# Graph layer kernel, last six steps of the table loop: another bank for the turned rows, another order of work on three engines

## The chip, the cores and the metric

One core of a Trainium2 chip runs the whole program, in one launch. The metric is the device time of one execution in microseconds (us), lower is better. Engines are called by the names that the profile gives them: PE (TensorE, matrix products; PEld are its weight loads), DVE (VectorE), ACT (ScalarE), POOL (GpSimd, which here above all issues indirect DMAs), SP (SyncE, which issues plain DMAs).

## The reference, cut to what matters

The input is x, 3125 nodes of 256 float32 values, with 50000 edges (sorted by target node), an edge type (one of 3) for each edge and a node type (one of 6) for each node. The result is x plus three layers:

```
xn = layernorm(x)
x  = x + gnn(xn) + mix(xn)
x  = x + ffn(layernorm(x))         # only for the half of the nodes with the largest gate

gnn:  K, Q, V = xn @ W[node_type] + b[node_type]         # 256 -> 256 each, a weight matrix for each node type
      per edge type t: score = (K[src] Wa[t]) . Q[dst] * pri[t] / sqrt(32), softmax over all edges of the type,
      message = weight * V[src] Wm[t]; summed by dst, plus xn, layernorm
mix:  q, k, v = xn @ Wqkv.T; q, k = elu + 1; kv = k'v by head; t = q kv / (q . sum k)
      x1 = layernorm(t + xn); y = gelu(x1 @ W1.T + b1) @ W2.T + b2; layernorm(y + x1)
```

The change touches how the node tables K, V and Q times Wa are made, and how the last tiles of the mix layer are laid between them. What is computed stays the same.

## The kernel before, in words

The program is written out engine by engine. Each engine has a fixed list of instructions, and the order between engines is kept by semaphores: `then_inc` on an instruction counts up when it has ended, and `wait_ge` holds the engine that issues it, and all that stands behind it in its list. There is no planner; the order is that of the Python loops.

The first part (up to line 1310) reads x, normalises it, sorts the nodes into tiles of one type each (`NS` = 30 tiles of 128 slots, since a type's last tile is not full), and then runs **the table loop**: 31 steps, s = 0 to 30. In step s each engine does its share of table tile s (and of its neighbours s+1, s-1), and of the mix layer's tiles, of which there are only `NT` = 25, in a pipeline of six stages: mix tile s enters in step s, and tile s-5 leaves. So from step 25 on no new mix tile enters and the pipeline drains; the last mix tile leaves in step 29.

A table tile's way, by its lines: POOL loads its rows by an indirect DMA (`load`, L618, two steps ahead). PE turns them (`turn_in`, L883, two transposes, one step ahead) into PSUM bank ps[0]; ACT copies them out (`turn_in` of ACT, L714). PE multiplies them with the type's key and value weights (`keys_values`, L908, four products into ps[1]); DVE adds the bias (`kv_out`, L1227); POOL stores the tile by an indirect DMA (`store_kv`, L629). ACT copies the type's query weights (`weights`, L722). PE forms the queries (`queries`, L919), also in ps[0]; DVE adds their bias (`q_bias_in`, L1237), signalling g_qc. One step later PE multiplies them with the blocks of the edge types (`by_type`, L896), ACT copies the result (`q_out`, L732) and POOL stores it (`store_q`, L635).

Since queries and turned rows share ps[0], PE's `turn_in` of tile s+1 waits for g_qc of tile s. 

A mix tile's way: `mix_q` (L947, ps[2]), ELU on ACT and DVE (L760, L763, L1258, the last signals m_kf), `mix_t` (L959, ps[5]), `attend` on DVE (L1267 to L1276), `roots` on POOL (L644, L645), `shift` (L1250, DVE), `centre` (L752, ACT), `mix_turn` (L983, into ps[6]), `affine` (L771, ACT), `mix_h` (L972, ps[7]), `gelu` (L781, ACT), `mix_y` (L993 and L994, into ps[6] again), `residual` (L1284 to L1287 on DVE, reads ps[6], its last operation signals m_c), `roots` again, `finish` (L1293 to L1299, DVE), then SP stores the tile (L523). Two waits matter here, since mix_turn and mix_y share ps[6]: in step s the `mix_turn` of tile s-2 and the `mix_y` of tile s-4 both wait for m_c of tile s-5, which comes from the `residual` of that same step s.

The order of work within step s on each engine, before the change:

```
PE    mix_q(s)  keys_values(s)  mix_t(s-1)  mix_turn(s-2)  queries(s)  mix_h(s-3)  turn_in(s+1)  by_type(s-1)  mix_y(s-4)
DVE   residual(s-5)  kv_out(s)  elu(s)  q_bias_in(s)  attend(s-1)  finish(s-5)  shift(s-1)
ACT   centre(s-2)  elu(s)  affine(s-2)  weights(s+1)  gelu(s-3)  turn_in(s+1)  q_out(s-1)
POOL  roots(s-5)  gained(s-2)  load(s+2)  store_kv(s)  roots(s-1)  store_q(s-1)
```

After the loop, POOL waits for the key and value stores and for SP's first `s_end` (all mix tiles stored), and begins **the edge stage**: for each of 98 groups of edges four indirect gathers of 128 rows (L1406), 392 in all, while DVE, PE and ACT form scores, exponentials and window sums. SP's second `s_end`, after the last query store has landed, lets the other engines in. Then come the sums by node, the layer norms, the selection of nodes and the feed-forward layer (L2226, L2236).

Of the kernel before, what the change touches and what calls it, by code (L numbers as in the profile page):

```python
# [11 lines left out]
ACT = mybir.ActivationFunctionType  # L12
# [3 lines left out]
P = 128  # L16
N, D = 3125, 256
# [4 lines left out]
NT = -(-N // P)  # L22
# [44 lines left out]
def build(nc, a, out):  # L67
# [13 lines left out]
    with ExitStack() as ctx:  # L81
# [23 lines left out]
        ident = sb("ident", [P, P])  # L105
# [97 lines left out]
        xg = edge.take(2, D)  # L203
        xgT = edge.take(2, D)
# [123 lines left out]
        ps = [psum[:, i * 512:(i + 1) * 512] for i in range(8)]  # L328
# [35 lines left out]
        def seen(eng, event, tile, unit=1):  # L364
            if tile is not None and isinstance(event, list):
                eng.wait_ge(event[tile.k], unit * (tile.i + 1))
            elif tile is not None:
                eng.wait_ge(event, tile.t + 1)
# [42 lines left out]
        def type_marks(c, dve, in_t, tmp):  # L411
# [25 lines left out]
        g_T, g_Tc, g_w, g_kv, g_kvc, g_q, g_qc, g_qp, g_qpc = (  # L437
            sem(n) for n in ("g_T", "g_Tc", "g_weights", "g_kv", "g_kvc", "g_q", "g_qc", "g_qp", "g_qpc"))
# [9 lines left out]
        late_vecs = [name for name in vec_names if name not in mix_vecs]  # L448
        N_BIAS, N_LATE = 2 * NTY + len(mix_vecs) + 1, len(late_vecs) + 3
        PARTS, BY_DVE = (0, 5, 10, 15, NT), 10  # L450
        N_ROWS = 2 + len(vec_names) + 2

        with nc.Block() as block:
# [90 lines left out]
            def _(pool):  # L544
# [80 lines left out]
                def store_kv(t):  # L625
                    if t is None:
                        return
                    seen(pool, g_kvc, t)
                    pool.indirect_dma_start(kv_d[:, :], where(t), tab_kv[:, t.k, :], None).then_inc(g_kvout[t.k], 16)  # L629
# [9 lines left out]
                def roots(t, ready, done, n):  # L639
                    if t is None:  # L640
                        return
                    seen(pool, ready, t)
                    j = 2 * n + t.k
                    cm(pool.tensor_scalar(rss[:, j, 1:2], mvs[:, j, 1:2], EPS_LN, None, ALU.add))  # L644
                    pool.tensor_tensor(rss[:, j, 0:1], rss[:, j, 1:2], nhalf[:, 0:1], ALU.pow).then_inc(done, 1)  # L645

                def gained(t):
                    if t is None:
                        return
                    if t.t == 0:  # L650
                        pool.wait_ge(s_pri, 1)
                    seen(pool, m_xh, t)
                    seen(pool, m_c, t.at(-3))
                    pool.tensor_tensor(x1g[:, t.t % 3, :], xh[:, t.k, :], vecs["L0_mix_ln1_g"][:, :], ALU.mult).then_inc(m_xg, 1)
# [2 lines left out]
                load(Tile(0, 1, NS))  # L657
                for s in range(NS + 1):
                    t, m = Tile(s // 2, s % 2, NS), Tile(s // 2, s % 2, NT)
                    roots(m.at(-5), m_c, m_r2, 1)  # L660
                    gained(m.at(-2))
                    load(t.at(2))
                    store_kv(t.at(0))
                    roots(m.at(-1), m_tx, m_r1, 0)
                    store_q(t.at(-1))
                seen_all(pool, g_kvout, NS, 16)
# [2 lines left out]
            def _(act):  # L669
# [39 lines left out]
                def turn_in(t):  # L709
                    if t is None:  # L710
                        return
                    seen(act, g_q, t.at(-2))
                    seen(act, g_T, t)
                    act.activation(xgT[:, t.k, :], ps[0][:, 0:D], ACT.Copy).then_inc(g_Tc, 1)  # L714

                def weights(t):
                    if t is None:
# [78 lines left out]
            def _(pe):  # L796
# [80 lines left out]
                def turn_in(t):  # L877
                    if t is None:
                        return
                    seen(pe, g_qc, t.at(-1))  # L880
                    seen(pe, g_in, t, 16)
                    for ch in range(C):
                        ins = pe.transpose(ps[0][:, ch * P:(ch + 1) * P], xg[:, t.k, ch * P:(ch + 1) * P], ident[:, :])  # L883
                    ins.then_inc(g_T, 1)

                def by_type(t):
# [13 lines left out]
                def keys_values(t):  # L900
                    if t is None:
                        return
                    ty = pe.value_load(slot_tyi[0:1, t.t:t.t + 1], min_val=0, max_val=NTY - 1)
                    seen(pe, g_Tc, t)
                    seen(pe, g_kvc, t.at(-1))
                    settle(pe)
                    for ch in range(C):
                        ins = pe.matmul(ps[1][:, :], xgT[:, t.k, ch * P:(ch + 1) * P],  # L908
                                        wall[:, ds(ty, 1), ch, 0:2 * D].rearrange("p a o -> p (a o)"),
                                        start=(ch == 0), stop=(ch == C - 1))  # L910
                    ins.then_inc(g_kv, 1)

                def queries(t):
                    if t is None:
                        return
                    seen(pe, g_w, t)
                    for o in range(C):
                        for ch in range(C):
                            ins = pe.matmul(ps[0][:, o * P:(o + 1) * P], wq[:, t.k, ch * D + o * P:ch * D + (o + 1) * P],  # L919
                                            xgT[:, t.k, ch * P:(ch + 1) * P], start=(ch == 0), stop=(ch == C - 1))  # L920
                    ins.then_inc(g_q, 1)
# [29 lines left out]
                def mix_t(t):  # L951
                    if t is None:
                        return
                    if t.t == 0:
                        pe.wait_ge(s_kvd, 1)
                    seen(pe, m_kf, t)
                    seen(pe, m_tx, t.at(-1))
                    for ch in range(C):
                        ins = pe.matmul(ps[5][:, ch * 132:(ch + 1) * 132], qf[:, t.k, ch * P:(ch + 1) * P], kvd[:, ch, :],  # L959
                                        start=True, stop=True)  # L960
                    ins.then_inc(m_t, 1)
# [35 lines left out]
                for s in range(NS + 1):  # L997
                    t, m = Tile(s // 2, s % 2, NS), Tile(s // 2, s % 2, NT)
                    mix_q(m.at(0))
                    if s == 0:  # L1000
                        state_by_values()
                    keys_values(t.at(0))
                    mix_t(m.at(-1))
                    mix_turn(m.at(-2))
                    queries(t.at(0))
                    mix_h(m.at(-3))
                    turn_in(t.at(1))
                    by_type(t.at(-1))
                    mix_y(m.at(-4))

            @block.vector
            def _(dve):
# [288 lines left out]

                for s in range(NS + 1):
                    t, m = Tile(s // 2, s % 2, NS), Tile(s // 2, s % 2, NT)
                    residual(m.at(-5))
                    ty = kv_out(t.at(0))
                    elu(m.at(0))
                    q_bias_in(t.at(0), ty)
                    attend(m.at(-1))
                    finish(m.at(-5))
                    shift(m.at(-1))  # L1310
# [1209 lines left out]
```

## Time and profile before

| | |
|---|---|
| median of 3 runs | 1071.82 us (1071.51 to 1072.44) |
| the profiled execution | 1069.83 us, of which the span in the trace is 1068.1 us |
| busy share of the span | PE 82%, DVE 75%, POOL 60%, ACT 55% |
| mean granted TensorE clock | 0.888 of full |
| table loop, first keys and values to last query store | 80.1 to 289.5 us |
| the six changed steps (25 to 30) | from 256.54 us on |
| edge stage, first gather to the last | 289.96 to 780.9 us |

How to read it: each part of the table is a stretch of the same trace, in us from the span's start. The stages follow one another, and only their seams overlap, so a high busy share over the whole span does not tell what a single stage is waiting for. In the views of the trace, a number in square brackets is the time that the engine sat idle before the instruction, and the name behind it is what ended that wait. "issue" means that the profile shows nothing that it waited for.

### The profile page before, as it was taken

What the parts mean: (1) busy time and instruction counts of PE and PEld (TensorE: products, weight loads), DVE (VectorE), ACT (ScalarE), POOL (GpSimd) and SP (SyncE); (2) the same over time, 40 slices, a digit from 0 to 9 for tenths busy, and PEclk for the clock granted to TensorE, in tenths of its full rate; (3) what the DMA queues carried; (4) which work ended last, traced back from release to release, by engine and by line L of the source; (5) the groups of instructions that cost most, each with busy time, mean ns of one, the idle gap of its engine ahead of it and who ended that gap; (6) DMA issues with size and microseconds to landing.
All of it is one profiled execution on the core that took longest, in us unless ns stands there. A gap on an engine that the chain in (4) does not pass through costs nothing. (4 is left out here: it accounts for less than half of the span.)

```text
span 1068.1 us, 18060 instructions
## 1 busy us (share of the span) xinstructions
PE 880.7 (82%) x5049; PEld 634.7 (59%) x5049; DVE 806.2 (75%) x1708; ACT 588.5 (55%) x1532; POOL 638.9 (60%) x818
## 2 busy tenths in 40 slices
PE   5999999999657877777777777778777948999998
PEld 3776877877434444444444444444447937888886
DVE  6754788888568889898888898988866837886541
ACT  2655999997346666666666666666641213223220
POOL 4615777878677777777777777777720047672000
PEclk9999999999958788888878888887868969999999
DMA  9722344444588888888888888888826332110020
GB/s 284 252 82 90 135 163 146 144 146 153 170 262 252 249 247 250 246 250 254 246 248 254 248 249 252 249 248 252 254 69 242 107 115 70 50 48 4 1 94 27
DMA packets 111497, 189.61 MB, mean 178 GB/s; under 512 B 17861, under 2 KB 80140, under 8 KB 111396
## 3 DMA queue, kind: packets, MB, share of 16 engines
q0 software_dynamic: 38896, 129.86, 39.2%
q1 hardware_dynamic: 69220, 55.29, 16.8%
q10 hardware_dynamic: 3280, 3.28, 0.9%
q8 instruction: 43, 0.70, 0.3%
q14 instruction: 58, 0.48, 0.1%
HBM read 154.21 MB, written 34.16 MB: 176 GB/s over the span
## 5 line engine op out<-in xcount | busy, mean ns | idle before, releaser
L1406 POOL DMA_INDIRECT big<-kv_scratch,src_i x336 | 318.7, 949 | 102.1 <-issue 100.3
L1563 PE MATMUL ps<-edge 64*128 64x256 f32 x784 | 151.3, 519 | 16.2 <-DMA edge<-q_scratch 12.8
L1579 PE MATMUL ps<-big,edge 128*64 128x256 f32 x672 | 118.3, 484 | 37.2 <-DVE big L1748 21.1
L1689 DVE TENSOR_TENSOR big<-big,ps 128x1024 f32<-128x1024 f32 x84 | 102.4, 1219 | 41.0 <-DMA big<-kv_scratch,src_i 37.2
L1563 PEld LDWEIGHTS ps<-edge 64*128 64x128 f32 x784 | 89.5, 246 | 58.2 <-issue 47.7
L1579 PEld LDWEIGHTS ps<-big,edge 128*64 128x64 f32 x672 | 52.7, 167 | 85.5 <-DVE big L1748 43.1
L1477 ACT ACTIVATE edge<-edge 128x64 f32<-128x64 f32 x392 | 102.9, 334 | 0.0
L1696 DVE TENSOR_REDUCE ps<-big 128x32 f32<-128x1024 f32 x84 | 102.5, 1220 | 0.1
L1748 DVE TENSOR_TENSOR big<-big,ps 128x1024 f32<-128x1024 f32 x84 | 99.1, 1213 | 0.0
L2160 ACT ACTIVATE big<-ps,fb 128x256 f32<-128x256 f32 (+2 forms) x104 | 39.5, 462 | 101.9 <-PE ps L2226 101.9
L2226 PE MATMUL ps<-big 128*128 128x256 f32 (+2 forms) x416 | 91.0, 376 | 2.7 <-ACT big L2147 2.7
L2236 PE MATMUL ps<-big 128*128 128x256 f32 (+1 forms) x400 | 90.2, 380 | 1.2 <-ACT big L2160 1.2
L1499 ACT ACTIVATE edge<-ps 128x256 f32<-128x256 f32 x98 | 37.6, 384 | 91.3 <-PE ps L1579 89.7
L2226 PEld LDWEIGHTS ps<-big 128*128 128x128 f32 x416 | 76.6, 198 | 11.9 <-ACT big L2147 3.6
L2236 PEld LDWEIGHTS ps<-big 128*128 128x128 f32 (+1 forms) x400 | 73.6, 188 | 12.0 <-ACT big L2160 1.4
L1597 PE MATMUL ps<-ones,edge 128*96 128x1 f32 x196 | 27.6, 244 | 54.6 <-ACT edge L1490 54.6
L1406 POOL DMA_INDIRECT wmix<-kv_scratch,src_i x56 | 53.0, 946 | 17.1 <-issue 17.1
L1597 PEld LDWEIGHTS ps<-ones,edge 128*96 128x96 f32 x196 | 23.7, 186 | 66.0 <-ACT edge L1490 66.0
L908 PE MATMUL ps<-big,edge 128*128 x120 | 56.9, 596 | 0.5 <-ACT edge L714 0.3
L1462 ACT ACTIVATE edge<-edge,iota_n 128x256 f32<-128x256 bf16 x98 | 48.7, 497 | 13.3 <-DMA edge<-key_scratch 13.2
L1465 ACT ACTIVATE edge<-edge,ones 128x256 f32<-128x256 f32 x98 | 49.8, 508 | 9.2 <-PE ps L1563 0.4
L1481 ACT ACTIVATE edge<-edge,ones 128x256 f32<-128x256 f32 x98 | 49.8, 509 | 8.9 <-ACT edge L1477 0.4
(353 smaller groups left out, 1895.8 us busy)
## 6 DMA issues: line engine op xcount, KB each, us to landing
edge<-q_scratch SPq DMA_DIRECT2D x196, 64.0 KB
edge<-key_scratch SPq DMA_DIRECT2D x98, 64.0 KB
big<-kv_scratch,src_i POOLq DMA_INDIRECT x336
agg_scratch<-big SPq DMA_DIRECT2D x16, 252.0 KB
xn_scratch<-big ACTq DMA_DIRECT2D x5, 640.0 KB, 6.6
mix_scratch<-big SPq DMA_DIRECT2D x25, 128.0 KB, 1.7
edge<-mix_scratch SPq DMA_DIRECT2D x1, 3200.0 KB, 12.7
big<-xn_scratch SPq DMA_DIRECT2D x25, 128.0 KB, 2.5
```

The lines of the kernel that those rows point to most:

```text
L908: ins = pe.matmul(ps[1][:, :], xgT[:, t.k, ch * P:(ch + 1) * P], wall[:, ds(ty, 1), ch, 0:2 * D].rearrange("p a o -> p (a o)"), start=(ch ...
L1406: pool.indirect_dma_start(kv_slots[s][:, k, :], None, kv_d[0:N, :], bass.IndirectOffsetOnAxis(ap=src_i[:, e:e + 1], axis=0)).then_inc(got[ ...
L1465: act.activation(ohT[:, g % 2, :], dist, ACT.Relu, bias=ones[:, 0:1], scale=-1.0).then_inc(oh, 1)
L1477: ins = act.activation(gap[:, 2 * k + hg, :], iota_m, ACT.Abs, bias=neg_key[:, e:e + 1])
L1563: ins = pe.matmul(qr_ps[g % 2][:, (2 * hg + k) * D:(2 * hg + k + 1) * D], ohT[64 * hg:64 * hg + 64, g % 2, k * P:(k + 1) * P], qwin[64 * h ...
L1579: ins = pe.matmul(sums_of(g)[64 * hg:64 * hg + 64, :], oneh[:, s, k, hg * 64:hg * 64 + 64], kv_slots[s][:, 2 * hg + k, D:2 * D], start=(k ...
L1597: ins = pe.matmul(z_ps[:, b:b + 1], ex[:, b % 2, u * 4 * TH:(u + 1) * 4 * TH], ones[:, 0:1], start=(u == 0), stop=(u == 1))
L1689: dve.tensor_tensor(k_rows, k_rows, qr_ps[g % 2].rearrange("p (k d) -> p k d", d=D), ALU.mult).then_inc(pr, 1)
L1696: dve.tensor_reduce(scr[:, g // 2 % 2, (g % 2) * EG * H:(g % 2 + 1) * EG * H].rearrange("p (k h) -> p k h", h=H), kv_slots[g % RING][:, :, ...
L1748: dve.tensor_tensor(v, v, wgt[:, g // 2 % 2, (g % 2) * EG * H:(g % 2 + 1) * EG * H] .rearrange("p (k h d) -> p k h d", h=H, d=1).to_broadc ...
L2226: ins = pe.matmul(hslot[q % 2][:, j * GT * P:j * GT * P + w], fw1[:, ch, f * P:(f + 1) * P], cols[:, ch, at:at + w], start=(ch == 0), stop ...
L2236: ins = pe.matmul(ps[4 + t % 2][0:m, 0:D], fh[:, p % 2, f, at:at + m], fw2[:, f, :], start=(f == 0), stop=(f == FJ - 1))
```

## The change

It applies to steps s >= `NT` = 25 alone; steps 0 to 24 stay as they are.

- Turned rows of table tiles 26 to 29 go to bank ps[2], where the mix layer's queries stood (last used for mix tile 24 in step 24). PE's `turn_in` for them waits for all ELUs (m_kf) in place of g_qc of the tile before; the wait for g_qc moves to `queries`.
- PE's order in steps 25 and later: `keys_values(s)`, `turn_in(s+1)`, `by_type(s-1)`, `queries(s)`, and then `mix_t`, `mix_turn`, `mix_h`, `mix_y`.
- DVE: `residual(s-5)` moves from the head of the step to behind `q_bias_in(s)`.
- POOL: `roots(s-5)` and `gained(s-2)` move behind `load(s+2)` and `store_kv(s)`.
- ACT's order is not touched; its copy only reads from the other bank.

```diff
+        def after_mix_q(t):
+            return t.t > NT
+
+        def turned_ps(t):
+            return ps[2] if after_mix_q(t) else ps[0]
...
@@ pool
                 for s in range(NS + 1):
-                    roots(m.at(-5), m_c, m_r2, 1)
-                    gained(m.at(-2))
+                    if s < NT:
+                        roots(m.at(-5), m_c, m_r2, 1)
+                        gained(m.at(-2))
                     load(t.at(2))
                     store_kv(t.at(0))
+                    if s >= NT:
+                        roots(m.at(-5), m_c, m_r2, 1)
+                        gained(m.at(-2))
                     roots(m.at(-1), m_tx, m_r1, 0)
                     store_q(t.at(-1))
...
-                    act.activation(xgT[:, t.k, :], ps[0][:, 0:D], ACT.Copy).then_inc(g_Tc, 1)
+                    act.activation(xgT[:, t.k, :], turned_ps(t)[:, 0:D], ACT.Copy).then_inc(g_Tc, 1)
...
@@ pe
                 def turn_in(t):
-                    seen(pe, g_qc, t.at(-1))
+                    if after_mix_q(t):
+                        pe.wait_ge(m_kf, NT)
+                    else:
+                        seen(pe, g_qc, t.at(-1))
                     seen(pe, g_in, t, 16)
...
                 def queries(t):
                     seen(pe, g_w, t)
+                    if after_mix_q(t):
+                        seen(pe, g_qc, t.at(-1))
...
                     keys_values(t.at(0))
+                    if s >= NT:
+                        turn_in(t.at(1))
+                        by_type(t.at(-1))
+                        queries(t.at(0))
+                        mix_t(m.at(-1))
+                        mix_turn(m.at(-2))
+                        mix_h(m.at(-3))
+                        mix_y(m.at(-4))
+                        continue
                     mix_t(m.at(-1))
...
@@ dve
                 for s in range(NS + 1):
-                    residual(m.at(-5))
+                    if s < NT:
+                        residual(m.at(-5))
                     ty = kv_out(t.at(0))
                     elu(m.at(0))
                     q_bias_in(t.at(0), ty)
+                    if s >= NT:
+                        residual(m.at(-5))
                     attend(m.at(-1))
```

## Rows read from the trace of the kernel before

**Rows 1.** The page: the span, and the clock in 40 slices.

```profile
span 1068.1 us, 18060 instructions
...
PEclk9999999999958788888878888887868969999999
```

**Rows 2.** The page, costliest groups: busy us, mean ns, idle before.

```profile
L1406 POOL DMA_INDIRECT big<-kv_scratch,src_i x336 | 318.7, 949 | 102.1 <-issue 100.3
...
L1406 POOL DMA_INDIRECT wmix<-kv_scratch,src_i x56 | 53.0, 946 | 17.1 <-issue 17.1
```

**Rows 3.** Windows, steps 27, 28, 29 with tail: PE, PEld, DVE, ACT, POOL, clock, DMA.

```profile
270.23:275.97 5.74, 5.74 (x35) 4.21 (x34) 3.80 (x9) 2.29 (x8) 3.86 (x6) 1.00 0.62 190
275.97:281.71 5.74, 4.96 (x28) 3.32 (x27) 3.82 (x9) 1.78 (x5) 2.86 (x4) 1.00 0.55 193
281.71:289.96 8.25, 4.54 (x29) 2.87 (x27) 3.82 (x9) 1.84 (x5) 5.03 (x9) 0.93 0.43 164
```

**Rows 4.** Timeline, step 28 on PE: start, us, engine line op, idle before.

```profile
275.97 1.88 PE L908 MATMUL ps<-big,edge 128*128 x4
...
277.69 1.05 PE L919 MATMUL ps<-edge 128*128 128x128 f32 x8
...
279.52 0.44 PE L883 MATMUL ps<-ident,edge 128*128 128x128 f32 x2 [0.78 <-DVE edge L1237]
...
280.74 0.70 PE L993 MATMUL ps<-wmix,big 128*128 128x256 f32 x2
...
281.71 1.88 PE L908 MATMUL ps<-big,edge 128*128 x4
```

**Rows 5.** Timeline, step 26: the residual's end, PE, ACT and DVE.

```profile
265.69 0.18 DVE L1287 BATCH_NORM_AGGREGATE big<-big 128x2 f32<-128x6 f32 x1
...
266.02 0.41 PE L983 MATMUL ps<-ident,big 128*128 128x128 f32 x2 [0.91 <-DVE big L1287]
266.27 1.06 PE L919 MATMUL ps<-edge 128*128 128x128 f32 x8
...
266.47 0.81 ACT L771 ACTIVATE big<-ps,ln1b,ln1g 128x128 f32<-128x128 f32 x2 [1.48 <-PE ps L983]
...
267.48 0.63 ACT L722 ACTIVATE edge<-big 128x512 f32 x1 [0.20 <-PE ps L919]
267.56 0.42 DVE L1237 TENSOR_TENSOR edge<-ps,big 128x256 f32<-128x256 f32 x1 [0.29 <-PE ps L919]
...
268.26 0.63 ACT L781 ACTIVATE big<-ps,b1c 128x128 f32<-128x128 f32 x2
...
268.77 0.38 ACT L714 ACTIVATE edge<-ps 128x256 f32<-128x256 f32 x1
```

**Rows 6.** Timeline, into step 25: the turned rows' copy, keys and values behind it.

```profile
255.86 0.38 ACT L714 ACTIVATE edge<-ps 128x256 f32<-128x256 f32 x1
...
256.54 1.98 PE L908 MATMUL ps<-big,edge 128*128 x4
```

**Rows 7.** Timeline, steps 29 and 30, up to the first gather.

```profile
281.91 0.43 DVE L1284 TENSOR_TENSOR big<-ps,big 128x256 f32<-128x256 f32 x1 [1.04 <-PE ps L994]
...
283.29 0.18 DVE L1287 BATCH_NORM_AGGREGATE big<-big 128x2 f32<-128x6 f32 x1
...
283.88 0.57 POOL L645 TENSOR_TENSOR big<-big,nhalf 128x1 f32<-128x1 f32 x1
...
286.37 0.92 PE L896 MATMUL ps<-big,edge 64*128 64x192 f32 x8 [1.04 <-ACT edge L732]
...
288.55 0.96 POOL L635 DMA_INDIRECT q_scratch<-edge,big  x1 [1.00 <-ACT edge L732]
...
289.96 1.02 POOL L1406 DMA_INDIRECT big<-kv_scratch,src_i  x1 [0.16 <-issue]
```

**Rows 8.** The page, DMA issues: the mix layer's stores, us to landing last.

```profile
mix_scratch<-big SPq DMA_DIRECT2D x25, 128.0 KB, 1.7
```

**Rows 9.** Windows of the edge stage around one fall of the clock.

```profile
514.00:517.40 3.40, 1.56 (x13) 1.10 (x12) 3.40 (x6) 1.87 (x7) 2.49 (x4) 1.00 0.87 248
517.80:524.20 6.40, 5.58 (x23) 3.05 (x25) 5.25 (x9) 3.77 (x11) 4.88 (x6) 0.50 0.82 248
```

More of the change, by code:

```diff
@@ L879, in turn_in @@
                         return
-                    seen(pe, g_qc, t.at(-1))
+                    if after_mix_q(t):
+                        pe.wait_ge(m_kf, NT)
+                    else:
+                        seen(pe, g_qc, t.at(-1))
                     seen(pe, g_in, t, 16)
                     for ch in range(C):
-                        ins = pe.transpose(ps[0][:, ch * P:(ch + 1) * P], xg[:, t.k, ch * P:(ch + 1) * P], ident[:, :])
+                        ins = pe.transpose(turned_ps(t)[:, ch * P:(ch + 1) * P], xg[:, t.k, ch * P:(ch + 1) * P], ident[:, :])
                     ins.then_inc(g_T, 1)
```

## The prediction, made before the changed kernel was run

> **What bounds the kernel now.** I read the stages first, then the seam between the table loop and the edge stage, then the changed steps instruction by instruction. The span and the clock line of the page [rows 1] show that no engine fills the whole span, so the worth of an edit has to be read where it lies. The edge stage is the long one, and POOL is what fills it: its 392 gathers are busy 371.7 us and idle 119.2 us in front of them, nearly all of it "issue", so one starts every 1.25 us with nothing else that it waits for [rows 2]. 392 times 1.25 is 491 us, the whole stretch from the first gather (289.96) to the last. Whatever moves the first gather therefore moves the end by as much: the rest of the program, POOL's gathers and what hangs on them, follows at a fixed distance.
>
> What sets the first gather is the table loop's end. It starts 1.41 us behind the start of the last query store, which came at once on ACT's copy of the last queries [rows 7]. Going back from there, steps 27 and 28 last 5.74 us each; in step 27 PE is busy throughout, in step 28 it idles 0.78 us [rows 3], in front of the turned rows, waiting for the bias of the queries, as both share a bank [rows 4]. That wait is what the change takes away. In step 26 another wait shows: PE's turning of mix tile 24 started 0.15 us after the end of the residual's statistics (L1287, signal m_c) [rows 5]. So m_c is already near PE's path when the residual stands first in DVE's list. Steps 25 and 26 together take 270.23 - 256.54 = 13.69 us [rows 3, 6].
>
> **The change, step by step.** Let K be the start of keys and values (L908) in a step. I lay the new order out with durations of the old rows.
>
> PE first does keys and values: 1.72 us until the next product starts (275.97 to 277.69). Then turned rows and types: 1.22 us (279.52 to 280.74). Then queries: 1.05 us, ending at K+3.99 [rows 4]. All this can run without a stop: the rows for the turn were gathered more than a step earlier, ps[2] has been free since step 24, and the types' copy by ACT stands behind a turned-rows copy that had to precede K. So the wait of 0.78 us is gone, and PE reaches the end of the queries as early as it can. The wait for g_qc that `queries` now makes is for a bias of the step before: free. In step 28 before, queries ended at K+2.77; now they end at K+3.99, behind the two moved parts.
>
> DVE adds the bias 0.23 us after the queries' end (266.27 + 1.06 to 267.56) and takes 0.42 us [rows 5]: K+4.64. Only then does it begin the residual, whose four dependent operations take 1.56 us (281.91 to 283.47) [rows 7]: m_c comes at K+6.20. Before, it came at K+1.76 (283.47 - 281.71) in step 29, since the residual was first. Moving it behind the bias is the edit that costs: `mix_turn` and `mix_y` of the same step wait for m_c, and on PE the next keys and values are queued behind them. PE goes on 0.15 us later, as in step 26 before [rows 5], at K+6.35.
>
> Steps 25 and 26. At K+6.35 PE turns a mix tile. ACT's order was not changed, and it holds the next turned-rows copy (which keys and values of s+1 need) behind affine, weights and gelu. From the turn's start: affine starts after 0.45 and takes 0.81, weights follow 0.20 later for 0.63, together 2.09 us; gelu then takes 0.51 until the copy starts [rows 5]; and 0.68 us from the copy's start to the next keys and values [rows 6]. `mix_h` (the same product shape as L919, 1.06 us) ends at 0.25 + 1.06 behind the turn, before gelu's place, so it is covered. 6.35 + 2.09 + 0.51 + 0.68 = 9.63 us a step, 19.26 for two against 13.69: **+5.57 us**. The cover of the weights' copy is gone here: before, it lay beside PE's work; now its 0.83 us is in the chain.
>
> Step 27. No mix tile is turned. `mix_h` ends at K+5.05, gelu and copy would allow the next start at K+6.3, but `mix_y` waits for m_c until K+6.35 and takes 0.97 us (280.74 to 281.71) [rows 4]: 7.32 against 5.74 us, **+1.58**. Step 28 is the same without `mix_h`: **+1.58**.
>
> Steps 29 and 30. No rows are turned, so PE ends the queries at 1.72 + 0.92 (types, by the duration of L896 [rows 7]) + 1.05 = K+3.69; bias to K+4.34, residual to K+5.90. POOL's list in step 29 has `roots` of the last mix tile in front of both last query stores. The roots end 0.98 us after m_c (283.47 to 284.45) [rows 7]: K+6.88. Then the first query store at about K+7.08 (an estimate of 0.2 us for the issue, from gaps of 0.16 to 0.30 us in [rows 2, 7]), the next 1.25 us later at the pace of [rows 2], K+8.33, and the gathers 1.41 us behind that, K+9.74. Against 8.25 [rows 3]: **+1.49**. PE's own route is shorter: types at K+4.4 plus 2.18 us to the store (286.37 to 288.55) [rows 7] is K+6.6. SP's first `s_end` also has to come: the last finish operation starts after the roots and takes about half a us, and the store lands after 1.7 us [rows 8], about K+9.3, just under K+9.74. It is the next to bind, and adds at most some tenths.
>
> Moves on POOL's queue: `load` and `store_kv` now pass `roots` and `gained`, which gives them up to 1.5 us more of a lead than they need. `roots(s-1)` of step 25 stands behind m_c, and `shift` and `centre` of tile 24 behind that, by some 4 us before the turn in step 26 wants them. Both are counted at nothing; the cover is the wait for m_c itself. SP's mix stores start later with `finish`; nothing reads them until the end.
>
> Sum at full clock: 5.57 + 1.58 + 1.58 + 1.49 = **+10.2 us**.
>
> **The clock** is the unknown term. Through the changed steps it was 1.00, with PE nearly always busy [rows 3]. In the new order PE stands still from K+3.99 to K+6.35, 2.4 us in steps 26 and 28 (less in 25, where `mix_t` fills 0.6, and 1.3 us in 27), and again 0.9 us at the end of steps 25 and 26. In the edge stage the clock fell from 1.00 to 0.50 after 3.4 us in which PE was busy 1.56 us, with no longer pause than about 2 us, and stayed at the lower of its two levels (1.2 for 2.4 GHz) for some 6.5 us [rows 9]. The page's clock line, down to 0.5 to 0.8 in the middle slices, says that this happens again and again there [rows 1]. So I expect falls here too. One of them costs half of the part of its 6.5 us that lies on PE's block of 4.0 us in a step of about 8.4: 6.5 / 2 x 4.0 / 8.4 = 1.5 us. With two falls: +3.1 us. Bounds: none, 0; four falls, one for each of the steps 25 to 28, 6 us. I take two, as two of the gaps are the long ones: **+13.2 us** in all.
>
> Here the Trainium skill gives a milder answer. Its page "TensorE: Matmul & The Clock Gate", section "HAM oscillation — how this bites in real kernels", names only pauses longer than any that I find in the new order as dangerous to the clock. By that rule the clock would hold, which is the first rival. The row above speaks against it.
>
> Against the profiled execution that is 1069.83 + 13.2 = 1083.0 us; its own time stood 2.0 us under the median of the runs (1071.82), so for the median I give 1071.82 + 13.2 = **1085.0 us**.
>
> **The rivals.**
>
> Clock holds. Everything as above with the granted clock at 1.00 from 256 to 290 us: +10.2, **1082.0 us**. For it: none of the table loop's short pauses before (0.78 us) lowered the clock. Against it: [rows 9]. Chance 0.24.
>
> The clock stays low through the drain. If PE at half clock never gets busy enough to be raised again, each of five blocks of 4.0 us nearly doubles: 10.2 + some 5 x 3 = +25, or with half of that, +18: **1090 us**. For it: slices with 0.5 [rows 1]. Against: after each fall PE has eight us of unbroken work. Chance 0.08.
>
> Faster, as the step by itself would be. If m_c were there before PE is through with the queries, PE would run without a stop: steps 27 and 28 at 1.72 + 1.22 + 1.05 + 0.97 = 4.96 us (`mix_h` more in 27), 0.78 less than before in step 28, and about 0.7 less in each of 25 and 26, where the turn waited on the residual: -2 to -3 us, **1069.5 us**. Place: m_c against K+3.99 in each step. It decides when the residual ends before that; but it can't begin before K+4.64 by DVE's list, so this needs a misreading of the order on my part. Chance 0.04.
>
> No change. The change doesn't do what its words say on ACT, where the copy stays behind gelu; if only the turned rows' wait and this were on the path, gain and loss could cancel; or the lost time could be hidden in front of the gathers. It would need slack in POOL's stage, and [rows 2] shows none. **1071.8 us**, chance 0.03.
>
> **How the numbers follow.** Forecast 0.61, clock holds 0.24, clock stays low 0.08, faster 0.04, no change 0.03. About 0.2%, 2.1 us, is what a measurement of this kernel can tell from no change. Faster 0.04, same 0.03, slower 0.93. The range leaves out the two cases without a loss and the upper end of the low clock. Its lower end is the clock-holds case less about 2.5 us for handovers shorter than the rows show (about ten of them by a quarter of a us); its upper end is 10.2 + 6 with 1 to 2 us for SP's signal and slower handovers: 1079.5 to 1089.5 us.
>
> **What the profile of the changed kernel would show.** L1284 of steps 25 to 29 starts behind L1237, not in front of L1227, and L983, then L993, wait on DVE L1287 by 1 to 2.4 us. The starts of L908 lie 9.6, 9.6, 7.3 and 7.3 us apart at full clock, and up to 2 or 3 us more where a fall hits. L883 no longer waits for L1237. The first gather starts at about 303 us, and the gathers keep 1.25 us. The granted clock between 257 and 300 us is under 1.00 in one or more stretches. I am wrong if L908's distances stay under 7 us (then m_c wasn't on the path), if ACT's L714 starts right after L883 in steps 25 and 26 (then gelu doesn't hold it), or if the edge stage takes up the delay.

## The result, and the profile after

| | before | changed |
|---|---|---|
| median of 6 runs, us | 1070.63 (1069.2 to 1072.44) | 1082.38 (1080.31 to 1084.36) |
| ratio to before | | 1.011, 95% interval 1.0091 to 1.0129 |
| profiled execution, us (span) | 1069.83 (1068.1) | 1084.36 (1082.6) |
| changed steps to the first gather, profiled | 33.4 us | 47.7 us |

The kernel became slower, by 11.75 us in the medians; 13.2 were forecast. The profiled execution of the changed kernel is the slowest of its runs, so its trace shows the worst case: 14.3 us more between the start of step 25 and the first gather. The median of the kernel before is now one of six runs; the first three of them gave the 1071.82 us that the forecast starts from. What follows is unchanged: POOL's 392 gathers keep their pace, as in [rows 2]. The page of the changed kernel, costliest groups (busy us, mean ns, idle before):

```profile
L1433 POOL DMA_INDIRECT big<-kv_scratch,src_i x336 | 318.3, 947 | 102.1 <-issue 100.9
L1433 POOL DMA_INDIRECT wmix<-kv_scratch,src_i x56 | 53.2, 949 | 17.1 <-issue 16.8
```

Lines have moved by 6 to 27: PE's L908, L919, L883, L896, L983, L993 and L994 of before are now L921, L934, L896, L909, L998, L1008 and L1009; DVE's L1227, L1237, L1284 to L1287, L1293 and L1299 are L1251, L1261, L1308 to L1311, L1317 and L1323; ACT's L714, L722, L732, L771 and L781 are L724, L732, L742, L781 and L791; POOL's L629, L635, L644, L645 and L1406 are L635, L641, L650, L651 and L1433. In kernels with fillers the later lines lie 7 to 11 further on.

The windows of the changed kernel, one row a step (25 to 28) and the last row for steps 29, 30 up to the first gather; they answer to [rows 3]. Columns: length, busy us of PE, PEld, DVE, ACT, POOL, granted clock, DMA.

```profile
257.71:267.27 9.56, 7.68 (x41) 5.52 (x42) 6.32 (x19) 3.76 (x11) 6.44 (x9) 0.91 0.41 139
267.27:277.63 10.36, 8.02 (x38) 5.35 (x38) 4.02 (x10) 3.46 (x10) 5.03 (x6) 0.83 0.31 104
277.63:285.69 8.06, 6.67 (x35) 4.32 (x35) 3.40 (x8) 2.85 (x8) 4.01 (x5) 0.90 0.40 128
285.69:293.24 7.55, 5.27 (x27) 3.26 (x27) 3.88 (x9) 1.26 (x3) 3.71 (x5) 0.97 0.30 110
293.24:305.43 12.19, 6.31 (x29) 3.39 (x28) 4.37 (x10) 1.75 (x4) 6.24 (x10) 0.78 0.29 110
```

The timeline of step 25 shows the new chain in order; it answers to [rows 4, 5]:

```profile
257.71 1.98 PE L921 MATMUL ps<-big,edge 128*128 x4
...
260.69 1.16 PE L934 MATMUL ps<-edge 128*128 128x128 f32 x8
...
262.08 0.42 DVE L1261 TENSOR_TENSOR edge<-ps,big 128x256 f32<-128x256 f32 x1 [1.47 <-PE ps L934]
262.43 0.42 DVE L1308 TENSOR_TENSOR big<-ps,big 128x256 f32<-128x256 f32 x1
...
263.80 0.18 DVE L1311 BATCH_NORM_AGGREGATE big<-big 128x2 f32<-128x6 f32 x1
...
264.13 0.41 PE L998 MATMUL ps<-ident,big 128*128 128x128 f32 x2 [1.83 <-DVE big L1311]
...
264.57 0.81 ACT L781 ACTIVATE big<-ps,ln1b,ln1g 128x128 f32<-128x128 f32 x2 [5.41 <-PE ps L998]
...
265.30 0.63 ACT L732 ACTIVATE edge<-big 128x512 f32 x1
...
265.83 0.61 ACT L791 ACTIVATE big<-ps,b1c 128x128 f32<-128x128 f32 x2
...
266.33 0.38 ACT L724 ACTIVATE edge<-ps 128x256 f32<-128x256 f32 x1
...
267.27 2.72 PE L921 MATMUL ps<-big,edge 128*128 x4
```

PE ends the queries, DVE idles 1.47 us for them, adds the bias, then does the residual, and PE idles 1.83 us for the residual's last operation. ACT, idle for 5.4 us, then takes affine, weights, gelu and copy one behind the other, and the next keys and values follow. That it is the copy which they wait for shows in a second trace of the same kernel (changed_again, below), where the clock stayed up in this step:

```profile
265.86 1.98 PE L921 MATMUL ps<-big,edge 128*128 x4 [0.43 <-ACT edge L724]
```

The last row of the first trace takes 2.72 us for four products instead of 1.98: the granted clock had fallen from 1.00 to 0.50. It did so three times before PE's last product of the stretch; the windows between a fall and the rise after it:

```profile
265.54:268.95 3.41, 3.41 (x6) 1.98 (x7) 1.70 (x6) 2.44 (x7) 2.44 (x4) 0.50 0.15 49
275.78:279.19 3.41, 3.40 (x6) 2.11 (x7) 0.54 (x1) 2.52 (x7) 1.71 (x2) 0.50 0.27 79
292.85:296.26 3.41, 3.41 (x6) 1.17 (x4) 0.58 (x2) 0.00 (x0) 1.86 (x2) 0.50 0.39 147
```

### The profile page after: what moved, and what is told of

It reads as the page before. It is cut to its first block and busy times, and to the rows that moved or that the text cites. A ratio compares the mean times of both kernels' runs of the same rounds, so it can differ in the third digit from the quotient of the medians.

```text
span 1082.6 us, 18064 instructions
## 1 busy us (share of the span) xinstructions
PE 888.4 (82%) x5049; PEld 637.9 (59%) x5049; DVE 806.4 (74%) x1708; ACT 586.7 (54%) x1532; POOL 641.3 (59%) x818
## 5 line engine op out<-in xcount | busy, mean ns | idle before, releaser
L1433 POOL DMA_INDIRECT big<-kv_scratch,src_i x336 | 318.3, 947 | 102.1 <-issue 100.9
L1606 PE MATMUL ps<-big,edge 128*64 128x256 f32 x672 | 121.3, 494 | 34.9 <-DVE big L1775 19.4
L1590 PEld LDWEIGHTS ps<-edge 64*128 64x128 f32 x784 | 89.7, 246 | 60.9 <-issue 46.1
L1433 POOL DMA_INDIRECT wmix<-kv_scratch,src_i x56 | 53.2, 949 | 17.1 <-issue 16.8
L921 PE MATMUL ps<-big,edge 128*128 x120 | 60.1, 625 | 0.5 <-ACT edge L724 0.3
```

Of the source, the lines that this page charges most:

```text
L1433: pool.indirect_dma_start(kv_slots[s][:, k, :], None, kv_d[0:N, :], bass.IndirectOffsetOnAxis(ap=src_i[:, e:e + 1], axis=0)).then_inc(got[ ...
L1590: ins = pe.matmul(qr_ps[g % 2][:, (2 * hg + k) * D:(2 * hg + k + 1) * D], ohT[64 * hg:64 * hg + 64, g % 2, k * P:(k + 1) * P], qwin[64 * h ...
L1606: ins = pe.matmul(sums_of(g)[64 * hg:64 * hg + 64, :], oneh[:, s, k, hg * 64:hg * 64 + 64], kv_slots[s][:, 2 * hg + k, D:2 * D], start=(k ...
```

## The experiments

Theory A was that the residual behind the bias makes m_c late, and that this wait, with ACT's chain behind it, is most of the loss. Theory B put it down to PE's new order itself, theory C to the clock alone. All times below are medians; "stretch" is the trace's time from the start of step 25 to the first gather (33.4 us before).

**residual_first**: one edit of the change undone.

```diff
-                    if s < NT:
-                        residual(m.at(-5))
+                    residual(m.at(-5))
                     ty = kv_out(t.at(0))
                     elu(m.at(0))
                     q_bias_in(t.at(0), ty)
-                    if s >= NT:
-                        residual(m.at(-5))
```

> The changed kernel with one edit undone: DVE's residual stands at the head of steps 25 and later again; PE's and POOL's new order and the bank stay. Theory A (the residual behind the bias makes m_c late, and that is most of the loss): m_c comes at about K+1.8 instead of K+6.2, PE turns the mix tile right behind the queries, steps 25 and 26 take 3.99 + 0.61 (mix_t, in 25 alone) + 2.09 + 0.51 + 0.68 = 7.9 and 7.3 us, step 27 6.3, step 28 5.0, and the tail loses its 1.5 us: +1.0 us against the kernel before, between 0 and +2. Theory B (it is PE's new order itself, with the mix layer's products last, whatever DVE does): steps stay at 9 us and more, +8 us or more. Theory C (the fallen clock alone): the pauses go with the late m_c, so it would look as under A in time, but the steps of the changed kernel that ran at full clock would have been short, which they were not.

Measured: 1071.63 us against 1070.3, ratio 1.001 (1.0001 to 1.0018), +1.3 us. Its windows, steps 25 to 28 and tail:

```profile
257.74:265.03 7.29, 6.80 (x40) 4.79 (x41) 5.58 (x17) 3.51 (x11) 5.62 (x9) 1.00 0.54 182
265.03:271.91 6.88, 6.35 (x37) 4.35 (x37) 4.53 (x12) 3.56 (x11) 5.40 (x7) 1.00 0.44 152
271.91:278.18 6.27, 5.90 (x35) 4.05 (x35) 4.05 (x11) 2.15 (x8) 4.19 (x5) 1.00 0.53 169
278.18:283.02 4.84, 4.84 (x27) 3.34 (x28) 2.47 (x7) 2.24 (x6) 2.64 (x4) 1.00 0.36 129
283.02:292.74 9.72, 4.74 (x29) 2.82 (x27) 5.12 (x12) 1.76 (x4) 5.40 (x10) 0.86 0.42 159
```

One edit takes back some nine tenths of the loss, with PE's new order in place, so theory B can't be most of it. PE's pauses are down to about half a us a step or less, and the clock is at 1.00 in all four. The new orders of PE and POOL are not free, though: against bank_only (below), which has the same bank with all orders as before, this kernel took 2.8 us more in the median and 35.0 against 32.3 us in the stretch. The tail missed: I had expected it to lose its excess, and it took 9.72 us. Its timeline shows two things, a late DVE and POOL's new order.

```profile
284.34 0.42 DVE L1308 TENSOR_TENSOR big<-ps,big 128x256 f32<-128x256 f32 x1
...
285.72 0.18 DVE L1311 BATCH_NORM_AGGREGATE big<-big 128x2 f32<-128x6 f32 x1
...
286.88 0.69 DVE L1251 TENSOR_TENSOR edge<-ps,big 128x512 f32<-128x512 f32 x1 [0.98 <-issue]
...
287.85 0.96 POOL L635 DMA_INDIRECT kv_scratch<-edge,big  x1 [3.32 <-DVE edge L1251]
288.05 0.92 PE L909 MATMUL ps<-big,edge 64*128 64x192 f32 x8 [1.21 <-DVE edge L1261]
...
288.84 0.24 POOL L650 TENSOR_SCALAR big<-big 128x1 f32<-128x1 f32 x1
...
289.93 1.09 POOL L641 DMA_INDIRECT q_scratch<-edge,big  x1 [0.20 <-ACT edge L742]
```

DVE still finished mix tile 23 when step 29 began at 283.02, so the last residual started 1.3 us into the step, and the bias of keys and values came 0.98 us behind its end, a gap for which the profile names no cause. POOL idled 3.32 us for that bias and only then did the roots (288.84 to 289.74), since the change had put them behind the store of keys and values. m_c had been there since 285.90, so in the old order they would have fitted into the idle time. By these rows the last store, started at 291.33, would have gone out some 0.8 us sooner, an estimate that no run tests.

**late_residual_27**: the same edit from the other side, put into the old order of PE from step 27 on, with the bank and with POOL's part of the change (`roots` and `gained` behind the stores), which the excerpt below doesn't show. In steps 25 and 26 it can't be put in: there the old order has `mix_turn` in front of `queries`, and `mix_turn` would wait for a residual that itself waits for the queries.

```diff
-                    residual(m.at(-5))
+                    if s < 27:
+                        residual(m.at(-5))
                     ty = kv_out(t.at(0))
                     elu(m.at(0))
                     q_bias_in(t.at(0), ty)
+                    if s >= 27:
+                        residual(m.at(-5))
```

> The kernel before with the other bank, PE's old order, and the one edit under test put in alone: DVE's residual behind the bias, with POOL's roots behind its stores, in steps 27 and later (in 25 and 26 the old order of PE would never get m_c). Theory A prices it: step 27 from 5.6 to 6.1 us, step 28 from 4.7 to 6.1, tail from 8.25 to 9.7, together +3.4 us over bank_only and +2 us against before. Theory B (the order on PE is what costs): nothing, as PE's order is the old one, -1.5 us against before.

Measured, on another chip: 1196.03 us against 1194.0, ratio 1.0019 (1.0005 to 1.0033). That chip runs the edge stage slower (in the trace, POOL idles 208 us before the first 336 gathers, against 102), and the table loop at the same pace, so I compare windows: step 27, 28 and tail of this kernel, then of bank_only.

```profile
270.23:276.80 6.57, 5.69 (x35) 3.99 (x34) 3.40 (x8) 2.30 (x8) 3.92 (x6) 1.00 0.70 209
276.80:283.06 6.26, 5.04 (x28) 3.21 (x27) 3.88 (x9) 1.74 (x4) 3.69 (x5) 1.00 0.35 128
283.06:292.73 9.67, 4.64 (x28) 2.97 (x28) 4.37 (x10) 1.75 (x4) 6.28 (x10) 0.94 0.37 142
```

```profile
271.38:277.01 5.63, 5.63 (x35) 4.18 (x34) 3.79 (x9) 2.29 (x8) 3.90 (x6) 1.00 0.58 191
277.01:281.75 4.74, 4.74 (x27) 3.29 (x26) 3.66 (x9) 1.78 (x5) 2.85 (x4) 1.00 0.51 185
281.75:290.00 8.25, 4.55 (x29) 2.87 (x27) 3.97 (x10) 1.84 (x5) 5.02 (x8) 0.96 0.50 192
```

0.94 + 1.52 + 1.42 = 3.9 us in three places, 3.4 expected. Removed or added, the late residual carries most of the loss. POOL's part is not told apart from it here; in residual_first it stayed in while nine tenths of the loss went.

**bank_only**: the kernel before with `turned_ps` and the two waits that go with it, all orders as before.

> The kernel before with the other bank alone (turned rows of tiles 26 to 29 in ps[2], without the wait for the bias), all orders as before. It measures what the bank is worth. Expected: the wait of 0.78 us in front of L883 in step 28 goes, nothing else, -0.8 us against before (between 0 and -1.5). If the bank held more than that, the other steps would shorten as well, by up to 2 us in all.

Measured: 1068.79 us against 1070.3, ratio 0.9988 (0.9976 to 1.0). Its windows above: step 28 takes 4.74 instead of 5.74 us, PE busy in all of it; the stretch is 32.3 us, 1.2 less than before. The bank is the part of the change that is worth something. The median's 1.5 us is at the edge of what can be told from nothing, the trace's is not.

**act_copy_first** and **act_copy_again**: the changed kernel with ACT's order changed.

```diff
                     centre(m.at(-2))
+                    if s >= NT:
+                        weights(t.at(1))
+                        turn_in(t.at(1))
+                        q_out(t.at(-1))
+                        affine(m.at(-2))
+                        gelu(m.at(-3))
+                        continue
                     elu(m.at(0))
```

> The changed kernel with ACT's order changed too: in steps 25 and later weights, the copy of the turned rows and q_out come before affine and gelu. It prices the copy's place. Theory A (m_c late, and behind it the chain over affine, weights, gelu and copy): in steps 25 and 26 PE binds from the mix tile's turn on, 6.35 + 1.3 + 1.0 = 8.6 us instead of 9.6, steps 27 and 28 stay at 7.3 us, since they wait for mix_y and not for the copy: 2 us less than the changed kernel, so +9 to +10 us against the kernel before. A rival, that the copy's place is the whole loss: steps of 6 us and about 0 us against before. Another, that ACT's chain is covered: no difference from the changed kernel, +11.7 us.

> ACT's copy of the turned rows in front of affine and gelu, beside the changed kernel on the same chip. In the first trace step 25, at full clock, took 8.71 us instead of 9.56, and the stretch to the first gather 46.1 us, but the medians did not differ. If the place of the copy is worth what step 25 shows, 1 to 2 us under changed_again; if falls of the clock take it back, within 1 us of it, with the products of keys and values slower in at least one step.

Measured: 1082.1 us (ratio 1.0115, 1.0097 to 1.0133) and 1082.24 us (1.011, 1.0092 to 1.0129): no gain on the changed kernel's 1082.38 and 1081.72, where 2 us, then 1 to 2, were expected. The windows of act_copy_again:

```profile
257.69:266.49 8.80, 6.92 (x40) 4.83 (x41) 5.58 (x17) 4.40 (x11) 5.79 (x9) 1.00 0.46 151
266.49:276.57 10.08, 7.80 (x37) 5.91 (x37) 4.74 (x12) 4.57 (x10) 6.88 (x9) 0.83 0.40 118
```

Step 25 at full clock is shorter by 0.5 us than the changed kernel's 9.31 (below); the chain is right about the direction, but 1.0 us was expected. Step 26 gave it back at a clock of 0.83. Both traces of this kernel have two falls before PE's last product, and stretches of 46.1 and 45.8 us. Whether the falls take back the whole gain in the timed runs stays open, as those carry no windows.

**residual_first_act**: both, residual first and ACT's copy first.

> Residual at the head again and ACT's copy of the turned rows (with weights and q_out) in front of affine and gelu in steps 25 and later. With an early m_c, residual_first left steps 25 to 27 bound by the copy behind gelu (7.29, 6.88, 6.27 us). If that is so, PE binds here: about 6.9, 6.3, 5.9 and 4.8 us, 1.4 us less than residual_first, so about 0 against before. If the copy's place was not what bound those steps, no difference from residual_first (+1.3 us). The tail keeps its 9.7 us: there DVE is late with the bias.

Measured: 1193.54 us against 1194.0, ratio 0.9991 (0.9978 to 1.0004). Steps 25 to 28 took 6.91, 6.24, 5.72 and 4.74 us, as expected within 0.2: with an early m_c, the copy's place behind gelu was the next thing that bound steps 25 to 27. The tail took 10.73 us, a us longer than in residual_first, with DVE late and POOL's roots behind the store of keys and values again; so much was not foreseen, and takes most of the gain.

**filled_pauses** and **filled_half**: filler products on PE in the pauses of the changed kernel, 3, 5, 2 and 5 in steps 25 to 28 in the first, 1, 2, 1 and 2 in the second, whose edit is shown. Their results are never read.

```diff
+                def fill(s):
+                    if s > 28:
+                        return
+                    pe.wait_ge(g_kvc, s + 1)
+                    for j in range({25: 1, 26: 2, 27: 1, 28: 2}[s]):
+                        pe.matmul(ps[1][:, :], ident[:, :], kv_bias[:, 0, :], start=True, stop=True)
...
                         mix_t(m.at(-1))
+                        if s != 27:
+                            fill(s)
                         mix_turn(m.at(-2))
                         mix_h(m.at(-3))
+                        if s == 27:
+                            fill(s)
                         mix_y(m.at(-4))
```

> The changed kernel with idle products on PE (128x512 into ps[1], after kv_out has read it, overwritten by the next keys and values; their result is never read): 3, 5, 1 + 1 and 5 of them in the pauses of steps 25, 26, 27 and 28, each 0.43 us. It tells the clock's share from the waiting's. If the falls of the clock cost what the trace of the changed kernel suggests, the granted clock stays at 1.00 from step 25 to 28, the distances of the starts of L921 are 9.6, 9.6, 7.3 to 7.5 and 7.3 to 7.5 us, and the time is 1 to 3 us under that of the changed kernel, so +9 to +11 us against before, with less spread between runs. If the clock costs nothing (the slower products are hidden), the time is that of the changed kernel, +11.7 us. If theory A is wrong and only the clock made the steps long, they come down to 6 us.

Measured: 1083.34 us (ratio 1.0121, 1.0106 to 1.0137), no faster than the changed kernel; the two intervals overlap. I had sized the fillers wrongly: one takes 0.86 us, not 0.43 (five end to end took 4.3 us), and five of them pushed `mix_turn` back (11.1 us for step 26). The clock did stay at 1.00 in all four steps.

> The fillers again, in half the number: each of them takes 0.86 us, not 0.43, so that filled_pauses overfilled the pauses. Now 1, 2, 1 and 2 of them in steps 25, 26, 27 (in front of mix_y) and 28. If it is right that the waiting is most of the loss and the clock the rest, the granted clock stays at 1.00 through steps 25 to 28, those four steps take 9.6, 9.6, 7.4 and 7.4 us (34.0 in all, where the profile of the changed kernel has 35.5), and the time is 1 to 3 us under the changed kernel's, +9 to +11 us against before. If a slower product costs nothing here, no difference from the changed kernel.

> The fillers beside the changed kernel on the same chip. The clock stays at 1.00 in steps 25 to 28, 44.0 us to the first gather, and 1 to 3 us under changed_again in the median. If the clock costs nothing on this path, no difference.

> The changed kernel itself, for more runs and a second trace beside the next two on one chip. The time between 257 us and the first gather was 47.7 us in the first trace, which was of its slowest run, with three falls of the clock in steps 25 to 29; by the fillers' 44.1 us at full clock the spread of its runs (1080.3 to 1084.4) would be that of how many falls there are and where they hit. So here 44.5 to 48 us, with one to three falls, and more spread between runs than filled_half has: 3 to 4 us. If the falls were an accident of that one trace, this one has none, and 44 us.

filled_half on the slower chip: 1207.09 us against 1194.0, ratio 1.0116 (1.0097 to 1.0134). On one chip: filled_half_again 1080.63 us, ratio 1.0098 (1.0083 to 1.0113); changed_again 1081.72 us, ratio 1.0111 (1.0096 to 1.0127). The windows of filled_half, steps 26 and 28; steps 25 and 27 took 9.31 and 7.36 us, also at a clock of 1.00:

```profile
265.87:275.18 9.31, 8.26 (x41) 4.97 (x41) 4.28 (x11) 3.41 (x11) 5.17 (x7) 1.00 0.34 114
...
282.54:289.89 7.35, 6.78 (x32) 3.82 (x31) 3.89 (x9) 1.26 (x3) 3.55 (x5) 1.00 0.30 114
```

And those of changed_again, steps 25 to 28 and tail:

```profile
256.55:265.86 9.31, 7.00 (x41) 4.82 (x41) 6.06 (x18) 3.51 (x11) 6.31 (x9) 1.00 0.45 143
265.86:275.20 9.34, 6.54 (x37) 4.37 (x37) 4.28 (x11) 3.44 (x11) 5.16 (x7) 1.00 0.37 113
275.20:282.58 7.38, 5.99 (x35) 4.12 (x35) 3.40 (x8) 3.13 (x9) 4.02 (x5) 1.00 0.43 142
282.58:290.10 7.52, 5.24 (x28) 3.23 (x27) 3.88 (x9) 1.26 (x3) 3.68 (x5) 1.00 0.29 110
290.10:300.81 10.71, 4.84 (x29) 2.92 (x28) 4.37 (x10) 1.76 (x4) 6.26 (x9) 0.87 0.33 125
```

This second trace of the changed kernel has no fall in the four steps, against my expectation of one to three: 44.3 us for the stretch, the same to 0.2 us as with fillers. Its one fall, at 298.1, comes after PE's last product of the tail (ended 295.7), where it costs the stretch nothing; the kernel before has such a one at 288.8. It is of the fastest of its five runs (1079.28 us), the first trace of the slowest of its six (1084.36 us, 47.7 us). So theory C falls: with the clock up, the loss is 44.3 - 33.4 = 10.8 us in the trace. In these two traces the clock adds 0 and 3.5 us on top. In the medians, changed_again is 1.1 us slower than filled_half_again, but their intervals overlap, so a mean cost of the clock is not shown. Nor are the falls the whole spread between runs: the two traces differ by 1.2 us before step 25 already.

**tuned_tail** and **bank_and_26**: the bank alone, with queries in front of `mix_turn` in step 26; tuned_tail also moves `by_type` to the front of step 29.

```diff
                     mix_t(m.at(-1))
+                    if s == NT + 1:
+                        queries(t.at(0))
                     mix_turn(m.at(-2))
-                    queries(t.at(0))
+                    if s != NT + 1:
+                        queries(t.at(0))
```

> An attempt to beat both kernels: the bank alone, with two small moves on PE: in step 26 queries come before mix_turn (which there waits for m_c, 0.9 us of pause in step 26 before), and in step 29 by_type of tile 28 comes before queries. Expected: step 26 from 7.0 to 6.1 us, tail from 8.25 to 8.0, both on top of the bank's 1.2 us: -2.4 us against before. It would be no better than bank_only (-1.5 us) if in step 26 ACT's chain (affine, weights, gelu, copy) sets the step.

> The other bank, and queries before mix_turn in step 26, without the move of by_type in step 29 (which made tuned_tail's tail 8.50 us instead of 8.25). Steps 6.65, 6.1, 5.6, 4.7 and tail 8.25, 31.4 us to the first gather against 33.4 of the kernel before: -2.0 us, and 0 to 0.5 us better than tuned_tail was (-2.5 us by its median, -1.8 by its trace). If the tail was an accident, no better than tuned_tail.

Measured: tuned_tail 1190.75 us against 1194.0, ratio 0.9979 (0.9964 to 0.9994), with a tail of 8.50 us, longer than before. bank_and_26 1068.11 us against 1070.6, ratio 0.9977 (0.9967 to 0.9986). Its windows of step 26 and of the tail:

```profile
265.92:272.03 6.11, 6.05 (x38) 4.36 (x37) 4.84 (x13) 3.33 (x10) 4.75 (x8) 1.00 0.48 162
...
282.40:290.65 8.25, 4.55 (x29) 2.88 (x27) 3.97 (x10) 1.84 (x5) 5.03 (x9) 0.98 0.51 196
```

Step 26 is down from 7.0 to 6.1 us with PE busy in nearly all of it, and the stretch is 31.4 us. This version beats both kernels: 2.5 us under the one before (0.2%, with an interval clear of 1), 13.6 under the changed one's median on the same chip. Whether it beats bank_only too, their medians, from two chips, don't show; the traces have 31.4 against 32.3 us.

## Why the prediction was right, and where its sizes were off

**What bounds the kernel: right.** The delay of the first gather went into the end nearly one to one: 15.5 us later in the first trace (1.2 of it from before step 25), 14.5 us more in the span. The last us is a later stage's.

**m_c late: right, and shown.** Forecast K+6.20, measured K+6.27 in step 25 (263.98 - 257.71), with PE going on 0.15 us later as forecast. Taking the edit out (residual_first) gave back all but 1.3 us of the loss against before, and putting it in with POOL's part cost 3.9 us in three places. The loss against the bank alone is larger, 44.3 - 32.3 = 12.0 us in the traces: 9.3 of it is the late residual (44.3 - 35.0), and 2.7 are the new orders of PE and POOL.

**Steps 25 and 26: 9.63 forecast, 9.31 and 9.34 at full clock.** The term was 0.3 us too long a step, since ACT's operations follow one another closer than the rows of step 26 before showed: from affine's start to the weights' it was 0.73 us (264.57 to 265.30) where before it was 1.01, with a wait of 0.20 for PE in it, and from the weights' to gelu's 0.53, less than the 0.63 counted. From the turn to the next keys and values it took 2.9 us (262.97 to 265.86 in changed_again), not 3.3.

**Steps 27 and 28: 7.32 forecast, 7.38 and 7.52 measured.**

**The tail: 9.74 forecast, 10.71 measured** in changed_again; the largest miss among the terms without the clock. Its end there, against [rows 7]:

```profile
295.97 0.18 DVE L1311 BATCH_NORM_AGGREGATE big<-big 128x2 f32<-128x6 f32 x1
...
296.19 0.49 DVE L1317 SCALAR_TENSOR_TENSOR big<-big,v_L_mix_ln_g 128x256 f32<-128x256 f32 x1
296.24 0.52 POOL L650 TENSOR_SCALAR big<-big 128x1 f32<-128x1 f32 x1 [2.00 <-DVE big L1311]
...
296.85 0.71 POOL L651 TENSOR_TENSOR big<-big,nhalf 128x1 f32<-128x1 f32 x1
...
297.65 0.49 DVE L1323 SCALAR_TENSOR_TENSOR big<-big,edge 128x256 f32<-128x256 f32 x1 [0.52 <-POOL big L651]
297.76 1.34 POOL L641 DMA_INDIRECT q_scratch<-edge,big  x1 [0.20 <-issue]
299.40 0.96 POOL L641 DMA_INDIRECT q_scratch<-edge,big  x1 [0.30 <-issue]
...
300.81 1.01 POOL L1433 DMA_INDIRECT big<-kv_scratch,src_i  x1 [0.16 <-issue]
```

m_c came at K+6.05 (5.90 forecast), the roots ended 1.41 us later (0.98), the two stores started 1.64 us apart (1.25), and the gathers 1.41 us behind the second, as forecast: 0.15 + 0.43 + 0.39 = 0.97 us.

**The sum at full clock** was +10.2; by the traces it is +10.8, with errors of both signs inside.

**The clock was over-sized.** I took two falls of 6.5 us on PE's path for +3.1 us. Measured: three falls before PE's last product in one execution and none in another of the same kernel, 3.4 us each where they came, and 3.5 us of time for three (47.7 - 44.3), 1.2 us for one on the average. The median holds about 1 us of it, an estimate from 11.75 - 10.8. That falls come and lengthen PE's path was right; their cost was over-sized, and the row of the edge stage was the wrong one to take a fall's length from: there PE was busy 5.58 of 6.40 us at the lower level, here all of the 3.41 us before each rise. And one row was too few: of the 32 falls between the first and the last gather of the kernel before, 15 lasted about 3.4 us and 17 about 6.8. The first rival, that the clock holds, gave 1082.0 us, 0.4 us from the measured median; the forecast's 1085.0 is 2.6 us from it. As gains over the kernel before, the two stand level: +10.2 and +13.2 us, against +11.75 measured. The rest of the difference between the two comparisons, 1.2 us, is the median of the kernel before, 1070.63 us in six runs and 1071.82 in three. The forecast's sum had a term too large (the clock) and one too small (the tail), and that they partly cancel was luck. The forecast also read the clock as 1.00 through all changed steps; the tail's row [rows 3] has 0.93, from the fall at 288.8 behind PE's last product. The Trainium skill's rule ("TensorE: Matmul & The Clock Gate", the section "HAM oscillation — how this bites in real kernels"), by which only longer pauses than these are dangerous, is not what the first trace shows: the clock fell with no pause above 2.3 us. In the second trace it held with the same pauses.

**The moves on POOL counted at nothing**: no run has them alone. In steps 25 to 28 of the changed kernel PE's waits name DVE and ACT, not POOL, and in its tail POOL idled 2.00 us for m_c in front of the roots, so that roots put earlier would not have started earlier. In residual_first, where m_c is early, they did bind the tail, as its rows show.

## What to carry to other kernels

Before an operation is moved behind another on one engine, follow its signal: a short one (1.6 us here) whose result another engine needs in the same step may be the wrong thing to call "work that can wait". Here its place cost 1 to 2.7 us a step, 9.3 us over five steps (changed_again against residual_first). A reorder of one engine's list has to be checked against the lists that were left alone: here ACT's copy stood behind work that the change had made late. Try the parts of a change singly; the part that only removed a shared bank was the one worth keeping.

## What the runs showed of the hardware that I had not expected

Two POOL operations were held up by DVE. POOL's L650 on a 128x1 tile takes 0.23 to 0.25 us mostly, but 0.52 us when DVE's L1317 started just before it (296.19 and 296.24 above), and it then ended 0.08 us after L1317. An indirect store on POOL takes 0.96 us alone and 1.34 us beside DVE's L1323; the 0.38 us more are the time from the store's start to L1323's end (297.76 to 298.14). The Trainium skill's page "SBUF — State Buffer", section "Who interferes with whom", says that a DVE instruction with two inputs in SBUF contends with a GpSimd instruction that reads SBUF. L1317 and L1323 are such instructions, and the trace agrees for L650; for the store the times fit, but no run isolates the cause. Moving the residual behind the bias had moved these pairs onto each other, right in front of the last stores, as `finish` now follows the residual at once in the last steps. In the kernel before, the same roots in step 29 ran beside no such instruction:

```profile
283.56 0.23 POOL L644 TENSOR_SCALAR big<-big 128x1 f32<-128x1 f32 x1 [0.54 <-DVE big L1287]
```

In steps 25 to 28 the same kernel had its clock fall three times in one execution and never in another, with pauses of PE of the same length (1.8, 2.3, 1.4 and 2.3 us) at the same places. Whether a pause lowers the clock can't be read from its length alone. And one of the chips ran the edge stage so much slower that the whole program took 1194 us instead of 1070, while the table loop kept its pace to 0.1 us in the steps that are alike (6.67 and 7.02 us for steps 25 and 26 of late_residual_27, 6.62 and 7.02 in bank_only). There the granted clock was lower too, 0.64 from 400 to 500 us in tuned_tail against 0.83 in the kernel before. Which came first, the slower stage or the lower clock, the runs don't show.
